# The first tile's adapter loaded in rows and transposed on TensorE, and a new order of work at the end

## What is computed

```python
x = x + einsum('bct,bcd->bdt', x, W0[cond])                # 16 matrices 32x32
base = einsum('bti,oi->bto', x, W) + b                     # W is 512x512
h = einsum('bti,bir->btr', x, A[adapter])                  # A: [512, 16] of an adapter
x = x + base + einsum('btr,bro->bto', h, B[adapter]) * 2   # B: [16, 512]
```

## Time and profile before

| | |
|---|---|
| median of three runs | 85.22 us |
| profiled execution | 85.35 us, span 83.6 us |
| TensorE busy | 79.6 us, 95% of the span |
| VectorE, ScalarE, GpSimd busy | 59.3, 52.0, 35.0 us |
| data read and written | 11.74 MB, 4.19 MB |

### The profile page before, as it was taken

How to read it: one execution, slowest core, us unless ns; L and a number is a source line. 1 busy time by engine, 2 the same in 40 slices (tenths; PEclk the granted TensorE clock), 3 DMA queues, 4 the chain that set the end, 5 groups by cost and what they waited for, 6 DMA issues and landing times.

```text
span 83.6 us, 1999 instructions
## 1 busy us (share of the span) xinstructions
PE 79.6 (95%) x521; PEld 71.8 (86%) x521; DVE 59.3 (71%) x154; ACT 52.0 (62%) x179; POOL 35.0 (42%) x75
## 2 busy tenths in 40 slices
PE   4999999999999999999999999999999999999970
PEld 2368688999899999999999999999999999999930
DVE  2048495885888787777878787888787777876540
ACT  1545757766566675958666666666685957669120
POOL 6128888844442617080715344342617080303000
PEclk9999999999999999999999999999999999999999
DMA  0999779899776768676586878676874734120333
GB/s 13 307 347 315 143 199 261 165 365 329 209 239 163 239 196 245 197 206 213 143 250 171 238 178 241 174 248 151 219 211 159 177 110 152 45 92 7 119 125 125
DMA packets 15997, 16.06 MB, mean 192 GB/s; under 512 B 10225, under 2 KB 10482, under 8 KB 15986
## 3 DMA queue, kind: packets, MB, share of 16 engines
q1 hardware_dynamic: 14016, 11.74, 47.4%
q0 software_dynamic: 1248, 4.06, 17.0%
q10 hardware_dynamic: 722, 0.14, 0.9%
HBM read 11.74 MB, written 4.19 MB: 191 GB/s over the span
## 4 chain that ended last, share of the span: by engine, by line
PE 85%; DMA 6%; ACTq 3%; ACT 2%; issue 1%; DVE 1%
PE z_ps L548 58%; PE z_ps L585 9%; DMA a_raw<-in_lora_a 6%; PE y_ps L596 4%; PE y_ps L600 4%; PE y_ps L598 4%; PE ht_ps L572 2%; ACTq L323 1%; PE z_ps L580 1%; PE ht_ps L626 1%; ACT L317 1%; PE y_last L608 1%; PE y_ps L608 1%; ACTq L313 1%; DVE y_sb L534 1%
## 5 line engine op out<-in xcount | busy, mean ns | idle before, releaser
L548 PE MATMUL z_ps<-wa,x_hi 128*128 128x288 f32 (+2 forms) x240 | 50.3, 301 | 0.0
L548 PEld LDWEIGHTS z_ps<-wa,x_hi 128*128 128x128 f32 x240 | 38.0, 188 | 1.8 <-issue 0.5
L548 PE MATMUL z_ps<-wa,x_lo 128*128 128x288 f32 (+2 forms) x120 | 35.5, 296 | 0.0
L548 PEld LDWEIGHTS z_ps<-wa,x_lo 128*128 128x128 f32 x120 | 22.6, 188 | 0.0
L291 POOL DMA_INDIRECT b_raw<-in_lora_b,b_index_slot x16 | 17.6, 1097 | 4.4 <-POOL b_index_slot L289 4.4
L300 POOL CAST m_hi<-m_raw 128x128 fp32r<-128x128 f32 x15 | 4.4, 293 | 31.5 <-ACT m_raw L337 31.5
L480 DVE TENSOR_TENSOR z_lo<-z_ps,z_hi 128x256 fp32r<-128x256 f32 x30 | 11.3, 420 | 6.4 <-ACT z_hi L381 6.4
L381 ACT CAST z_hi<-z_ps 128x256 fp32r<-128x256 f32 x30 | 9.7, 376 | 9.7 <-PE z_ps L585 9.6
L337 ACT COPY m_raw<-w_raw 32x32 f32 x64 | 13.8, 216 | 1.8 <-DVE w_raw L502 1.2
L439 DVE TENSOR_TENSOR x_lo<-x_raw,x_hi 128x512 fp32r<-128x512 f32 x14 | 9.7, 690 | 3.5 <-ACT x_hi L349 3.5
L460 DVE TENSOR_TENSOR b_lo<-b_raw,b_hi 128x512 fp32r<-128x512 f32 x15 | 10.4, 693 | 1.6 <-ACT b_hi L369 1.1
(11 more groups left out here) (51 smaller groups left out, 78.8 us busy)
## 6 DMA issues: line engine op xcount, KB each, us to landing
out<-y_sb SPq DMA_DIRECT2D x15, 256.0 KB, 2.4
x_raw<-in_xt SPq DMA_DIRECT2D x14, 256.0 KB, 2.9
a_raw<-in_lora_a SPq DMA_DIRECT2D x60, 32.0 KB
first_sb<-in_first SPq DMA_DIRECT2D x2, 384.0 KB, 4.0
first_sb<-in_first SPq DMA_DIRECT2D x3, 256.0 KB, 4.8
b_raw<-in_lora_b,b_index_slot POOLq DMA_INDIRECT x16, 4.0
bias_sb<-in_bias SPq DMA_DIRECT2D x1, 256.0 KB, 5.2
out<-y_sb SPq DMA_DIRECT2D x2, 128.0 KB, 1.7
```

Source lines behind the costliest of these rows:

```text
L548: done = nc.tensor.matmul(target, (x_lo if lo_x else x_hi)[s][:, k, :], moving(lo_w), start=first and not lo_x and not lo_w, stop=last and ...
```

## The change

It has five parts.
1. PE's products without effect read the program's constant of one instead of `zeros`; nothing has to be set for them, and the ninth has 384 columns instead of 256.
2. A of tile 0 is loaded in another layout: 16 rows of 2048 bytes for each sample, into `a0_rows` [64, 512]. PE turns it with four transposes (into `y_last`), placed between `first_chunk(1)` and `first_chunk(2)`, and ACT copies the result from PSUM into `a0_sb`.
3. The piece with x of tile 1 is cut in two; the second half is issued behind A of tile 1. ACT and DVE take A of tile 1 before that half.
4. `b_index` is computed by DVE, between the identities of chunk 1 and the rest of chunk 0.
5. The end: tile 14's transposition, `mix(13)`, and `lora(14)` move ahead of the last two chunks of tile 15's first half; `mix(14)` and `lora(15, 0)` move ahead of chunk 2 of the second half. The first 256 columns of tile 15 are now split and mixed in three products; the other 256 stay in float32 but go in two parts of 128 columns. The last part is stored from ACT's queue.

```diff
-    WARM_UP = (512,) * 8 + (256,)
+    WARM_UP = (512,) * 8 + (384,)
-    PIECES = (0, X0_AT[1], W_AT[2], W_AT[3], X1_AT, X1_AT + T)
+    PIECES = (0, X0_AT[1], W_AT[2], W_AT[3], X1_AT, X1_AT + T // 2, X1_AT + T)
+    PARTS = (slice(0, HALF), slice(HALF, HALF + P), slice(HALF + P, O))
...
@@ SP
-            for n in range(len(PIECES) - 1):
+            for n in range(PIECE_OF_X1[0] + 1):
                 load_first(n)
             sp.wait_ge(ids_loaded, 16)
             load_a(1)
+            load_first(PIECE_OF_X1[1])
             load_x(2)
@@ ACT
-                act.dma_start(a_raw[0][:, j:j + 1, :, :].rearrange("p j k r -> p j (k r)"),
-                              lora_a[bass.ds(slot, 1)].rearrange("s p k r -> p s (k r)")
-                              ).then_inc(a_loaded[0], 16)
+                act.dma_start(a0_rows[j * R:(j + 1) * R, :],
+                              lora_a_rows[bass.ds(slot, 1)].rearrange("s r t -> (s r) t")).then_inc(a0_loaded, 16)
...
+            act.wait_ge(a0_transposed, 1)
+            act.copy(a0_sb[:, :, :], a0_in_psum(slice(0, KC))).then_inc(a0_ready, 1)
             round_x1(0)
-            act.wait_ge(a_loaded[0], 16 * J)
-            act.copy(a0_sb..., a_raw[0]...).then_inc(a0_ready, 1)
+            round_a(1)
             round_x1(1)
-            round_a(1)
...
             build_m(LAST - 1)
-            build_m(LAST)
-            round_h(LAST)
             for half in range(2):
                 round_z(LAST - 1, half)
-
-            for half in range(2):
-                act.wait_ge(lora_done, 2 * LAST + half + 1)
-                act.copy(z_sb[:, cols(half)], z_of(LAST, half)).then_inc(z_copied, 1)
+            round_h(LAST)
+            build_m(LAST)
+            round_z(LAST, 0)
+            act.wait_ge(lora_done, 2 * LAST + 2)
+            for n in range(2):
+                act.copy(z_sb[:, n * P:(n + 1) * P], z_of(LAST, 1)[:, n * P:(n + 1) * P]).then_inc(z_copied, 1)
+            act.wait_ge(y_ready, LAST + len(PARTS))
+            act.dma_start(out_rows[LAST * P:(LAST + 1) * P, PARTS[-1]],
+                          y_sb[LAST % 2][:, PARTS[-1]]).then_inc(last_part_stored, 16)
@@ DVE
             add_identity(0)
-            for k in range(KC - 1):
+            add_identity(1)
+            index_b()
+            rest_w(0)
+            for k in range(1, KC - 1):
                 add_identity(k + 1)
                 rest_w(k)
             rest_x1(0)
+            rest_a(1)
             rest_x1(1)
-            rest_a(1)
             rest_w(3)
@@ PE
+            first_chunk(0)
+            first_chunk(1)
+            pe.wait_ge(ident_ready, 1)
+            pe.wait_ge(a0_loaded, 16 * J)
             for k in range(KC):
-                first_chunk(k)
+                last = nc.tensor.transpose(a0_in_psum(k), a0_rows[:, k * P:(k + 1) * P], ident[0:JR, 0:JR])
+            last.then_inc(a0_transposed, 1)
+            first_chunk(2)
+            first_chunk(3)
             pe.wait_ge(a0_ready, 1)
```

More of the change, by code:

```diff
@@ L14, with lora_residual_program @@
 ALPHA = 32
-def lora_residual_program(nc, first, xt, ids_row, ids_of_p, w0, bias, lora_a, lora_b, out):
+def lora_residual_program(nc, first, xt, ids_row, ids_of_p, w0, bias, lora_a, lora_a_rows, lora_b, out):
     _, _, KC, _ = xt.shape
@@ L250, in _ @@
             store_y(LAST - 1)
-            for half in range(2):
-                sp.wait_ge(y_ready, LAST + 1 + half)
-                sp.dma_start(out_rows[LAST * P:(LAST + 1) * P, cols(half)],
-                             y_sb[LAST % 2][:, cols(half)]).then_inc(y_stored[LAST % 2], 16)
+            for n, at in enumerate(PARTS[:-1]):
+                sp.wait_ge(y_ready, LAST + 1 + n)
+                sp.dma_start(out_rows[LAST * P:(LAST + 1) * P, at],
+                             y_sb[LAST % 2][:, at]).then_inc(y_stored[LAST % 2], 16)
             sp.wait_ge(y_stored[0], 16 * (TILES // 2))
             sp.wait_ge(y_stored[1], 16 * (TILES // 2 + 1))
+            sp.wait_ge(last_part_stored, 16)
         @block.gpsimd
@@ L305, in _ @@
                 gather_b(u)
-            for u in range(LAST):
+            for u in range(TILES):
                 split_m(u)
@@ L314, in _ @@
             act.dma_start(ids_p_sb[:, :], ids_of_p).then_inc(ids_p_loaded, 16)
-            act.wait_ge(zeros_ready, 1)
-            act.copy(scratch[:, :], zeros[:, 0:1])
+            act.copy(scratch[:, :], nc.const_aps.tensor(1.0, (P, 1), BF16))
             adapters0 = [act.alloc_register(f"adapter0_{j}") for j in range(J)]
@@ L522, in _ @@
             rest_h(LAST - 1)
+            mask_ht(LAST - 1)
             rest_b(LAST)
-            mask_ht(LAST - 1)
             finish_y(LAST - 2)
-            rest_h(LAST)
             rest_z(LAST - 1, 0)
             rest_z(LAST - 1, 1)
+            rest_h(LAST)
             mask_ht(LAST)
             finish_y(LAST - 1)
+            rest_z(LAST, 0)
             dve.wait_ge(y_stored[LAST % 2], 16 * (LAST // 2))
[L532 to L535, removed]
+            for n, at in enumerate(PARTS):
+                dve.wait_ge(y_computed, LAST + 1 + n)
+                nc.vector.tensor_tensor(y_sb[LAST % 2][:, at], y_part(n), bias_sb[:, at], ALU.add).then_inc(y_ready, 1)
         @block.tensor
         def _(pe):
-            pe.wait_ge(zeros_ready, 1)
             for columns in WARM_UP:
-                nc.tensor.matmul(ht_ps[:, 0:columns].rearrange("p (a c) -> p a c", c=P), zeros[:, :],
-                                 zeros[:, :].rearrange("p (a c) -> p a c", a=1).broadcast_to([P, columns // P, P]),
-                                 start=True, stop=True)
+                nc.tensor.matmul(ht_ps[:, 0:columns], nc.const_aps.tensor(1.0, (P, P), BF16),
+                                 nc.const_aps.tensor(1.0, (P, columns), BF16), start=True, stop=True)
             def products(u, k, target, moving, first, last):
@@ L601, in mix, with mix_last_half, mix_last_quarter @@
                                  skip_group_check=True).then_inc(y_computed, 1)
[L603 to L609, removed]
+            def mix_last_half():
+                s = LAST % 2
+                pe.wait_ge(z_hi_ready, 2 * LAST + 1)
+                pe.wait_ge(m_ready, LAST + 1)
+                pe.wait_ge(y_ready, LAST - 1)
+                nc.tensor.matmul(y_part(0), m_hi[s][:, :], z_hi[s][:, cols(0)], start=True, stop=False,
+                                 skip_group_check=True)
+                nc.tensor.matmul(y_part(0), m_lo[s][:, :], z_hi[s][:, cols(0)], start=False, stop=False,
+                                 skip_group_check=True)
+                pe.wait_ge(z_ready, 2 * LAST + 1)
+                nc.tensor.matmul(y_part(0), m_hi[s][:, :], z_lo[s][:, cols(0)], start=False, stop=True,
                                  skip_group_check=True).then_inc(y_computed, 1)
+            def mix_last_quarter(n):
+                pe.wait_ge(z_copied, n + 1)
+                nc.tensor.matmul(y_part(1 + n), m_raw[LAST % 2][:, :], z_sb[:, n * P:(n + 1) * P], start=True,
+                                 stop=True, skip_group_check=True).then_inc(y_computed, 1)
             def first_chunk(k):
@@ L654, in _ @@
             last_chunk(1, 0)
+            transpose_h(LAST - 1)
             mix(LAST - 2)
-            transpose_h(LAST - 1)
+            lora(LAST - 1, 0)
+            lora(LAST - 1, 1)
             last_chunk(2, 0)
             last_chunk(3, 0).then_inc(main_done, 1)
-            lora(LAST - 1, 0)
-            lora(LAST - 1, 1)
             last_chunk(0, 1)
@@ L703 @@
         "lora_a": lora_a.reshape(-1, KC, P, R).transpose(0, 2, 1, 3),
+        "lora_a_rows": lora_a.transpose(0, 2, 1),
         "lora_b": _np.asarray(inputs["L1_cond_lora_Bs"]),
```

45 lines of the change are left out of this document (23 added, 22 removed).

## The result

The changed kernel takes 86.44 us (median of 5 timed runs) against 85.40 for the kernel before in the same session: ratio 1.0112, 95% interval [1.0082, 1.0143]. I had forecast 84.9 with a range to 85.7. It is slower by 1.1% and outside the range. The ratio leaves out runs over 1.5% above the kernel's fastest; here these are the two in which TensorE's clock fell, and the profiled run, 88.46 us with a span of 86.7, is one of them, so the start is shown once more under e9, whose profiled run was free of that.

A forecast was written before the change was run, and what follows sets the result against it. PE was taken as the bound, busy 79.6 of 83.6 us. +0.3 (A), -0.14 (B) and -0.45 (end) were summed to -0.3 us, taking the median from 85.22 to 84.9 us, range 84.2 to 85.7.

The forecast's parts named there:

- Part 2: At the start, loading A in rows with transposes between chunks: tile 1 begins at 10.9 instead of 10.61, +0.3 us.
- L: Time at which A of tile 0 has landed: taken as 7.8 us, range 7.4 to 8.2, break-even 7.5.
- L + 3.1: Start of tile 1 on PE: landing of A plus transposes, two chunks and products with A; not before 10.50.
- A stays late: Rival at the start: A lands at 8.6 or later, tile 1 begins at 11.7, +1.1, time 85.7; chance 0.15.
- The rule on taking turns between queues: DMA engines alternate between queues packet by packet, so A at the start would wait for about four of SP's packets.
- Part 1: At the start, products without effect need no zeros: at most 0.06 us gained, counted as 0.
- Part 3: At the start, the cut piece of x and the earlier split of tile 1's A: gain 0.
- Part 4: At B of tile 0, an earlier gather removes a small wait: -0.14 us, at most -0.22, at least 0.
- Part 5: At the end, reordered work, split products and a smaller last store: -0.45 us, between -0.1 and -0.65.
- The smaller last store: At the end, the last store of 64 KB instead of 128: -0.15 us, between 0 and -0.3.
- The clock: Rival at the start: the clock rises later or falls in the wait and transposes, time 86.6; chance 0.05.

The follow-up runs named there:

- e9: The changed kernel with `b_index` computed on POOL again; 86.37 us, ratio 1.0105 to the kernel before.
- e3: The kernel before with only the new end added; 84.92 us, ratio 0.9969.
- e7: The changed kernel with A of tile 0 loaded as before, without transposes, and x of tile 1's 256 KB piece uncut; 84.95 us, ratio 0.9982.
- e2: The changed kernel with A of tile 0 loaded as before in runs of 256 bytes, without transposes; 85.86 us, ratio 1.0052.
- e6: e2 with `b_index` on POOL again; 84.63 us, ratio 0.9935 to the kernel before.
- e14: e6 with A of tile 2 issued ahead of x of tile 2 and w0; 85.79 us, ratio 1.0087 to the kernel before.
- e1: The changed kernel with PE's four transposes of A behind all four first chunks; 85.45 us, ratio 1.0018 to the kernel before.
- e4: The changed kernel with eight products without effect, 512 columns each, ahead of PE's wait for A; 86.30 us, ratio 1.0124 to the kernel before.
- e5: The changed kernel measured again, nothing altered; 86.43 us, ratio 1.0153 to the kernel before.
- e8: The changed kernel with A of tile 1 issued only after A of tile 0 has landed; 91.34 us, ratio 1.0693 to the kernel before.
- e10: e9 with the transposes behind all four first chunks; 85.52 us, ratio 1.0001 to the kernel before.
- e15: The same kernel as e4, measured again; 86.41 us, ratio 1.0141 to the kernel before.
- e16: e10 with A of tile 0 issued on both queues ahead of two pieces, two of tile 1's A transfers moved to ACT's queue; 85.85 us, ratio 1.0068.
- e12: e6 with A of tile 0 issued on both queues ahead of two pieces, two of tile 1's A transfers moved to ACT's queue; 85.67 us, ratio 1.0011.
- e13: e12 with A of tile 2 issued ahead of x of tile 2 and w0; 86.48 us, ratio 1.0079 to the kernel before.
- e11: e9 with tile 0's A read from fixed adapters 0 to 3, issued without waiting for the ids; 85.95 us, ratio 1.0068 to the kernel before.

## Why the prediction was wrong

*Where the time went.* e9's profile against that of before: tile 1 starts 12.20 - 10.61 = 1.59 later; the spans are 84.7 and 83.6, so the rest gave 0.5 back. The timed ratio (1.0105, +0.9) agrees.

*Part 2, the step that failed: the size of L.* Tile 1 was to begin at L + 3.1, and I took L = 7.8, having written that the trace has no such transfer; it was 9.17 and 9.13 in the two profiles of the changed kernel and 8.75 in e9. The first half of the way from 9.11 to it, 0.37 us for the 128 KB taken out from ahead of A, held about: in runs of 256 bytes L is 9.11, 8.92 and 8.74 with that piece ahead (before, e3, e7) and 8.39, 8.25 and 8.52 without (e2, e6, e14), some 0.5 in the mean. Its second half, a further 0.94 for 64 long runs instead of 512 short ones, was a guess by the nearest row, and nothing of it came: in rows L is 9.17, 9.03, 8.43, 9.13, 8.61, 8.75, 8.32 and 8.91 (changed, e1, e4, e5, e8, e9, e10, e15), 8.8 in the mean, against 8.4 in short runs; with A ahead it is 7.54 against 7.08 and 6.91 (e16 against e12, e13). The single values spread (8.32 to 9.17 against 8.25 to 8.52) and overlap, one profile each, and six of the eight in rows have part 4 but only one of the three in short runs; without part 4 it is 8.75 and 8.32 against 8.25 and 8.52. That rows bring no 0.94 us is shown; that they lose 0.4 is not.

*The rest of that step.* I had L + 3.1; in e9 it is L + 3.45: 0.14 from the landing to the first transpose (I had 0.05), transposes 0.43 by the chain (0.42), the chunks 1.92 (1.72; six of the eight steps are 0.22, but the first, and the one from the last pass to the products, are 0.3), the products 1.02 (0.9), less 0.06. Small terms, 0.35 together, and all the same way. With L = 8.8 tile 1 begins at 12.2, which is e9's. The form "one for one behind L" was right, and e1 and e10 show it by taking it away.

*The rival "A stays late"* was this case. I had given it 0.15, and its price too low: with L + 3.45 and the mean L of 8.8 tile 1 begins 1.64 later than before, and by my own -0.14 and -0.45 that is 86.3 in place of 85.7. Its support stood in the rows: both queues took 4 to 5 us alike. For 7.8 spoke one row of another shape, size and place, the first piece with nothing ahead.

*The rule on taking turns between queues* (the Trainium skill, DMA: Bandwidth & Descriptors, "Queues, rings and completion order") would have let A, alone on ACT's queue, pass SP's pieces. The trace of the changed kernel agrees in part. The four transfers of A are issued at 2.75 to 4.26 and take
```profile
DMA to landing us min/median/max: 3.9/4.3/4.9
```
so the first is in at 6.6 and the third at 8.1, while SP's third to fifth piece, all issued before any of them (1.74 to 2.68), land at 6.9, 7.8 and 8.2. A overtakes pieces ahead of it, but the last of A, for which PE waits, comes 1 us behind them all. And what is ahead on SP's queue still counts: e11's A, the last issued 0.5 us after SP's fifth piece, took 5.07 us; e12's and e16's landed 1.3 us earlier when 384 KB were put behind it, and 384 KB at 0.35 MB a microsecond are 1.1 us.

*Part 1.* 0, right within what can be seen; PE takes the first piece at 4.32 and 4.54 in the two profiles of the changed kernel (4.66 before) and does not wait at 1.06 any more.

*Part 3.* Costed at nothing. Its effect on L, counted under part 2, is real, and with A as before it seems to reach the time: e6 (with parts 1 and 3 beside 5) is 0.9935 where e3 is 0.9969, though the intervals overlap.

*Part 4.* I had -0.14 and named `rest_w(0)` and `round_w(2)` as what could be late. Neither was. The wait at B that it was to remove was real, 0.13 us (from the start of the product ahead of it 0.35 us before, 0.22 in e9), but e9 and e6, without part 4, have lost it too. In the changed kernel it gives nothing to be seen (e9), with part 3 and the start of before it costs 1 us (e2 against e6), through A of tile 2, a transfer that the prediction doesn't name. The earlier gather puts its bytes into the same stretch; whether that is the cause was not tried apart.

*Part 5.* -0.45 forecast, -0.26 [-0.52, -0.01] measured (e3). The chain from the last `lora` to the last DVE operation shrank by 0.28 (I had 0.3), and there was no wait for POOL. The smaller last store, -0.15, gave nothing: 2.2 us from its issue to the end of the span in both kernels, and 1.8 from issue to landing against 1.7 for 128 KB.

*The clock.* Given 0.05. It fell in both profiled runs of the changed kernel, 0.7 and 0.1 us after the transposes that follow the pause. Counting the changed kernel (twice) and e9, which have this pause and no filling, 6 of 24 runs lie above 87.5; e1 and e10, where all chunks come ahead of it, none of 24; with filling (e4, e15) none of 12; but e11 has the pause (1.61 us) and none either in 11 (a twelfth, at 130.9, is a disturbance of another kind), and e13 has three of 8 at 87.8 to 88.3 without it (it has a wait of 1.4 us at tile 2; e12, with 2.3 there, has none in 12). e8, with three pauses, has a fall in five of six, in its profile after the pause of 1.66 us at tile 1 and with no transposes near. That the pause makes a fall possible is likely and not shown. The Trainium skill (TensorE: Matmul & The Clock Gate, "Part 4: PE-mode transpose") says that transposes don't count as activity; the falls right behind them would agree, but the profiled runs of e9, e4 and e15 have the same four and kept it, and e8's fell elsewhere, so these runs neither need the rule nor exclude it.

## What to carry to other kernels

A wait in the middle of an engine's program costs whatever stands behind it; before moving one ahead of ready work, ask what is the latest time at which the awaited thing has been seen to land, and count from that. When a stretch is filled with transfers, look at the bytes issued ahead: earlier issue (e11), less traffic behind (e8) and another shape moved A's landing by no more than its spread, and putting other pieces behind it moved it by 1.3 us (e12, e16). But an issue takes time too: A of tile 2, moved ahead of x, delayed x by the 1.9 us that SP needs for A's four issues (e13, e14). Undo the parts one by one even where a change fails: three of the five together gave 84.63 us, 0.65% below the kernel before.

## What the runs showed of the hardware

- 128 KB in 64 runs of 2 KB landed no earlier than in 512 runs of 256 bytes, in the same place of the queue (8.8 against 8.4 us in the mean, 8.32 to 9.17 against 8.25 to 8.52).
- Four transfers of 32 KB took SP 1.90 us to issue (e13, e14), 0.5 each, and the transfer behind them was late by that, while the DMA engines were not full (busy for 0.31 of the time from 8 to 9 us in e13).
- The rise of the clock at the start comes at other times in other executions of nearly the same program: PE's passes change pace at 6.85 us before, and were fast from the first chunk on in the changed kernel's profile (eight passes in 2.15 us from 4.32). Before, the landing of A at 9.11 hid the difference.
- A store of half the size ended no earlier: 2.2 us from issue to the end of the span for 64 KB as for 128 KB; to the landing 1.7 (SP's queue) and 1.8 (ACT's) against 1.7.
